# Stores of the result begun by SP, behind the restack of the same slot, instead of by ScalarE

## The reference

```python
x = x + _L0_conv_ref(_gn(x), weight_int8, scale_weight, bias)       # quantized 3x3 convolution
x = x + _L1_conv_ref(_gn(x), w_real, w_imag, b_real, b_imag)        # in _L1: X = rfftn(x), 3x3 complex
                                                                    # convolution of X, bias, irfftn
```

## Time and profile before

| | |
|---|---|
| runs | 3467.41, 3472.81, 3480.56 us, median 3472.81 |
| profiled execution | 3469.19 us, of which 3467.5 us from the first to the last instruction |
| PE busy | 3194.4 us (92%) |
| DVE busy | 2965.4 us (86%) |
| ACT busy | 1908.3 us (55%), without the time its sequencer spends on DMAs |
| POOL busy | 2004.5 us (58%) |
| granted TensorE clock, mean | 0.962 of 2.4 GHz |

### The profile page before, as it was taken

One profiled execution on the slowest core, in us unless ns is written; L12 is line 12 of the kernel. 1 busy time (PEld: TensorE's weight loads), 2 busy tenths in 40 slices (PEclk: granted clock), 3 DMA queues, 4 the chain that ended last, 5 costly groups with the idle time before them and its releaser, 6 DMA issues.

```text
span 3467.5 us, 125723 instructions
## 1 busy us (share of the span) xinstructions
PE 3194.4 (92%) x45156; PEld 2630.8 (76%) x45156; DVE 2965.4 (86%) x5369; ACT 1908.3 (55%) x2831; POOL 2004.5 (58%) x2961
## 2 busy tenths in 40 slices
PE   6988884799999999999999999999999999999998
PEld 3544442488888888888888888888888888888888
DVE  7999998688888888888888888888888888888886
ACT  7999996344444444444444444444444444444443
POOL 3777400256666666666666666666666666666654
PEclk8999997799999999999999999999999999999999
DMA  8777763267777777777767777777777777777765
GB/s 309 245 244 243 240 240 99 67 208 213 211 212 211 217 213 221 215 214 218 217 210 217 216 216 211 219 213 213 220 214 212 212 219 215 212 210 216 218 192 179
DMA packets 545362, 735.72 MB, mean 212 GB/s; under 512 B 80272, under 2 KB 485872, under 8 KB 529296
## 3 DMA queue, kind: packets, MB, share of 16 engines
q1 hardware_dynamic: 351248, 467.90, 40.9%
q0 software_dynamic: 46080, 125.89, 13.8%
q10 hardware_dynamic: 147456, 134.28, 13.6%
HBM read 266.07 MB, written 135.79 MB: 116 GB/s over the span
## 4 chain that ended last, share of the span: by engine, by line
PE 52%; DVE 16%; DMA 6%; issue 5%; SPq 3%; POOL 1%; ACT 0%; DVEq 0%; ACTq 0%; POOLq 0%
PE y_ps L1084 15%; PE x_ps L1071 8%; PE conv_ps L1116 7%; PE fin_ps L1103 6%; DMA stack<-xn 6%; PE t_ps L1062 4%; DVE img L916 4%; SPq L513 3%; PE conv_ps L1118 3%; PE fin_ps L1098 2%; DVE y_lo L909 2%; PE mean_b L1127 2%; DVE img L926 2%; DVE xn L903 1%; DVE bn L918 1%
## 5 line engine op out<-in xcount | busy, mean ns | idle before, releaser
L601 ACT ACTIVATE xt<-t_ps 128x512 f32<-128x512 f32 x512 | 305.7, 597 | 999.4 <-PE t_ps L1062 910.2
L1084 PE MATMUL y_ps<-mix_w,stack 128*128 128x64 f16 x24576 | 811.7, 194 | 18.8 <-DMA stack<-xn 18.1
L1084 PEld LDWEIGHTS y_ps<-mix_w,stack 128*128 128x128 f16 x24576 | 792.7, 99 | 36.0 <-DMA stack<-xn 26.6
L794 POOL DMA_DIRECT2D img<-in_x x960 | 530.3, 553 | 462.0 <-DMA out<-img 404.8
L804 POOL TENSOR_SCALAR eo<-img,norm 128x256 f32<-128x256 f32 x512 | 477.9, 933 | 368.2 <-PE t_ps L1062 200.5
L916 DVE SCALAR_TENSOR_TENSOR img<-conv_ps,cst,img 128x512 f32<-128x512 f32 x512 | 383.2, 748 | 221.6 <-PE conv_ps L1118 216.4
L1071 PE MATMUL x_ps<-dft,xt 128*128 128x128 f32 x4096 | 562.1, 282 | 0.0
L1071 PEld LDWEIGHTS x_ps<-dft,xt 128*128 128x128 f32 x4096 | 518.5, 199 | 0.0
L594 ACT ACTIVATE scaled<-img,b,a 128x512 int16<-128x512 f32 x512 | 412.3, 805 | 96.7 <-DMA img<-in_x 40.8
L1103 PE MATMUL fin_ps<-inv,y_hi 128*128 128x128 f16 x4096 | 461.2, 222 | 0.0
L1116 PE MATMUL conv_ps<-quant,conv_w 128*128 128x512 f16 x1536 | 422.1, 384 | 34.8 <-DVE quant L897 25.7
(11 more groups left out here) (146 smaller groups left out, 5187.6 us busy)
## 6 DMA issues: line engine op xcount, KB each, us to landing
stack<-xn SPq DMA_DIRECT2D x2048, 132.0 KB, 3.3
out<-img ACTq DMA_DIRECT2D x1024, 128.0 KB, 3.4
img<-in_x SPq DMA_DIRECT2D x120, 1024.0 KB, 4.9
img<-in_x POOLq DMA_DIRECT2D x960, 128.0 KB, 3.4
halo<-quant SPq DMA_DIRECT2D x192, 193.3 KB, 4.2
halo<-quant SPq DMA_DIRECT2D x64, 169.1 KB, 3.9
img<-in_x SPq DMA_DIRECT2D x64, 128.0 KB, 2.7
kept<-rmx SPq DMA_DIRECT2D x32, 48.0 KB, 4.5
```

Of the source, the lines that this page charges most:

```text
L794: pool.dma_start(img[u][:, hb, :], src[:, :, hb, :]).then_inc(pair_s[u][j], 16)
L1084: last = nc.tensor.matmul(y_ps[t % 2][:, g, b, :], stack[:, t % 2, g, first:first + F], mix_w[:, 2 * at + b, g, f, part, :], start=i == 0, ...
```

## The change

The procedure `store` moves from ACT's program to SP's, unchanged but for the engine. In a slot it stands last, after that slot's restack; in the next slot halo rows, where there are any, come after it and before the next restack. Waits, destinations, sizes and semaphores are the same.

```diff
@@ SP
+            def store(s, u, t):
+
+                sp.wait_ge(done_s, done(s, t))
+                sp.sem_inc(tick_s, 1)
+                dst = out[s].rearrange("c (h r) w -> c r h w", r=R)
+                for hb in (2 * t, 2 * t + 1):
+                    sp.dma_start(dst[:, :, hb, :], img[u][:, hb, :]).then_inc(store_s[t % STORES], 16)
...
                     if runs(mix, conv, t + 3):
                         restack(s, t + 3)
+                    if mix and t >= 1:
+                        store(s, u, t - 1)
+                    if later(s, mix) and t == 0:
+                        store(s - 1, 1 - u, PAIRS - 1)
...
             periods(sp, period)
+            store(samples - 1, 1, PAIRS - 1)
@@ ACT
-            def store(s, u, t):
-
-                act.wait_ge(done_s, done(s, t))
-                act.sem_inc(tick_s, 1)
-                dst = out[s].rearrange("c (h r) w -> c r h w", r=R)
-                for hb in (2 * t, 2 * t + 1):
-                    act.dma_start(dst[:, :, hb, :], img[u][:, hb, :]).then_inc(store_s[t % STORES], 16)
...
-                    if mix and t >= 1:
-                        store(s, u, t - 1)
-                    if later(s, mix) and t == 0:
-                        store(s - 1, 1 - u, PAIRS - 1)
...
             periods(act, period)
-            store(samples - 1, 1, PAIRS - 1)
```

## The result

The changed kernel takes 3641.44 us (median of 3 runs, 3633.74 to 3642.38) against 3472.81: ratio 1.0477, 95% interval [1.0438, 1.0515]. It is slower by 168.6 us, where 4 were forecast and the range ended at 3512.

A forecast was written before the change was run, and what follows sets the result against it. PE was taken as the bound (92% busy), with little waiting within reach. Terms -4 + 9 - 5 + 4 = +4 us on the profiled 3469.2 gave 3473; runs' median stands 3.6 higher, so 3477 us, range 3450 to 3512.

The forecast's parts named there:

- SP becomes the bound in the halo slots: Rival, chance 0.33: restacks of slots 4 and 8 land 1.2 us late and SP carries the rest along; +35 us, 3508.
- In a quiet slot ... 4.4, against 4.71: it fits: SP's slots without halo rows: restack plus two store issues need 3.9 to 4.4 us, within PE's 4.71 us slot.
- The halo slots: SP's slots with halo rows: next restack starts 1.2 us later, landing put at 0.3 us later, giving +9 us.
- 31 waits: PE's waits for restacks, taken to show about half of such places, 62 over 31 samples, have no slack.
- In such slots the gain is nothing: ACT's sequencer, freed of 1.27 us a slot: PE's wait covers it; gain only once a sample, -4 us.
- +9 us and -5 us, the transfers: Restacks on SP's queue: +9 us from later landings behind halo rows, -5 us where they lose the store as rival.
- +4 us, bounds 0 and +25, for later loads: Stores landing 2.2 to 3 us later delay POOL's loads and ACT's scaled; +4 us was to reach PE.
- ACT's own idle time covers that: ACT's 1.82 us idle a slot was to absorb scaled's waits for late loads of some tenths to 1 us.
- The signs given: Profile signs: PE's stack wait 15 to 30 us if right, over 40 in many slots if wrong on the slow side.
- B: Theory tested in the follow-ups, not forecast: the stores' data stand in SP's queue ahead of the restacks.
- A: Theory tested in the follow-ups: SP's issue time is used up, so restacks and halo rows start late.
- C: Theory tested in the follow-ups: later stores make loads late, and so ACT's scaled and DVE's quant.

The follow-up runs named there:

- one-DMA store: Changed kernel with each store on SP as one DMA of 256 packets, result rows permuted: 3533.7 us; 3474.4 when loads also wait for no store.
- a dose of 270 us of waits: Kernel before, with POOL's loads also waiting for ACT's x_high of pair t+2: 3578.2 us, ratio 1.0294.
- four small DMAs: Kernel before, with four extra DMAs of 16 x 1 KB on SP behind each restack, stores still on ACT: 3889.3 us, ratio 1.1194.
- late loads: Kernel before, with POOL's load also waiting for the mixing of its slot: 3738.0 us, ratio 1.0769.
- three and four small DMAs: Kernel before, with three or four extra DMAs of 16 x 1 KB on SP behind each restack: 3685.95 us with three, 3889.3 with four.
- free loads: Stores read a constant and POOL waits for done_s, so no load waits for a store: 3452.5 us with stores on ACT, 3592.2 on SP.
- the faster version: Kernel before, with ACT's store called one place earlier, ahead of y_high: 3449.9 us, ratio 0.9924.

## Why the prediction was wrong

The direction was that of the rival *SP becomes the bound in the halo slots*, whose 3508 us was too small as well. Its mechanism, late halo slots carried along by SP, was in the main the right one, though it too left out the wait for halo rows; its size was not. Point by point:

- **"In a quiet slot ... 4.4, against 4.71: it fits"** is the step that failed. The sum left out most of SP's own steps. In the rows above the restack is followed by 0.34 us (0.26 in the median), not 0.05, a figure for which no row stands, and a further 0.25 us pass before the next restack: 2.77 + 0.34 + 1.39 + 0.25 = 4.75 us. The pair of stores took 1.38 us in the median, not 1.27. Over the loop a slot in which SP had no pause lasts 4.82 us, not 4.4. These steps are not busy time and stand in no row of an engine, but the earlier trace rows had one: 1756.89 - 1756.70 = 0.19 us between restack and halo rows. The one-DMA store (0.77 us less: 1.39 of the rows above against 0.62) brings that slot to 4.27 us and 139.7 us of loss to 21.9; that is the evidence. A resource needed for 4.82 of 4.71 us carries each delay on, instead of absorbing it in the next slot. (That the wait for `done_s` is free held: 97% of the pauses between restack and store stayed under 0.5 us.)
- **The halo slots** were costed for the restack only (1.2 us later). For one halo slot that was about right: 5.93 us between the restacks, 1.2 over PE's slot. With the lateness carried into it, the restack stood 2.1 us later behind its mixing than before in slot 4 (2.68 against 0.54) and 2.6 in slot 8 (3.38 against 0.77). Nor do the "31 waits" say that half of these places have no slack: of the 31 only 11, with 5.3 of the 18.1 us, are for restacks of slots 4 and 8. And the halo rows also start behind the store, and the convolution of the next slot waits for them: 54.7 us in the change, 82.5 where no load was late. The prediction has them end at 1759.4, later than before, and puts no price on it. I had asked what is queued behind the new wait and stopped at the next restack, though the queue's order has the halo rows first.
- **"In such slots the gain is nothing", -4 us for ACT** was about right as far as it was tested: 0.6 of ACT's 1.27 us less in each slot was worth 0 (ratio 0.9997).
- **+9 us and -5 us, the transfers.** Restacks did land sooner after their issue (median over the span 2.6 us against 3.3, stores 3.0 against 3.4), as forecast for a queue with no rival beside it. It did not matter: they were issued later by more. The other half of that step, shorter issues once ACT's are gone, did not come in the halo slots for which it was counted: the four issues of slot 4's restack take 3.11 us before and 3.10 after (medians). Over all slots they take 2.78 and 2.55. The restack issues of the changed kernel, beside the earlier trace rows:

```profile
L521 SPq DMA_DIRECT2D stack<-xn x2048: 529/600/2303, 669.1 to 3618.1; - x187
```

  600 ns against 606 in the median, 2303 against 2297 at most. What makes the issues of slot 4 long was not found; it is not ACT's stores. The lock on the descriptor generator, which the prediction had cited from the Trainium skill (Perfetto Trace Analysis, "DMA Instruction — HWDGE (DVE, Sync)"), can at most explain the 0.23 us between those two medians of all slots.
- **+4 us, bounds 0 and +25, for later loads** was mis-sized. The mechanism was right, ACT's wait went from 40.8 to 149.5 us. Inside the change it cost 28.9 us (give or take 18), and 39 (give or take 13) where SP was hardly in its way; a dose of 270 us of waits cost +103. "ACT's own idle time covers that" held for ACT, not for DVE, whose wait for `scaled` rose by 89 us.
- **The signs given** were met on the slow side: a `stack` wait over 40 us (79.3), the halo restack late, by 2.1 us instead of 1.2, loads and stores waited for more, the statistics' wait unchanged at 65.3 us.
- **Why the parts don't add.** PE's 4.71 us slot, SP's 4.82 and DVE's (2104 of 2465 us busy) lie close together. When SP makes PE late by a microsecond, a load gets that microsecond too; this is my reading. That both costs hide each other partly is measured: +415 us with four small DMAs, +264 with late loads, +463 with both.

What stays open: 41.4 us of the loss are PE's busy time, which did not rise at all with free loads (3201.8 and 3202.2 us). Late loads are not needed for such a rise: with three and four small DMAs, where the loads were not late, PE was busy for 3247.2 and 3303.4 us, 52.8 and 109 more than before. The mean granted clock was 0.954 in the change, 0.952 and 0.943 in those two, 0.962 before, and 0.959 and 0.963 with free loads. A clock of 0.954 in place of 0.962 would make 27 us of the 41.4, if all of PE's busy time went with it (an estimate, 3194.4 x 0.962 / 0.954 - 3194.4). What lowered it was not isolated, nor is it sure that the 28.9 us of the late loads hold none of it. Nor was B alone measured; after A and C there is little left for it, as the one-DMA store with free loads is within 22 us of its base with all the data in SP's queue. The Trainium skill (DMA: Bandwidth & Descriptors, "Issuing engines are not separate DMA queues") says that starting DMAs on several engines saves only sequencer time, which is usually small beside the DMA. These runs agree with the first half. The second is not so here: the 1.39 us of issuing two stores stand beside 3.0 us until one has landed, and on SP they were worth 139.7 us.

## What to carry to other kernels

Before you move a DMA, write the receiving sequencer's whole slot: from the start of one group of DMAs to the start of the next, gaps and waits included, and set it against the slot of the busiest engine. Here 4.82 us against 4.71 cost 139.7 us, and 4.27 still cost some 22; nothing between was measured. Where it comes near the other slot, count it as full, and count every delay in the longer slots as carried on until the next slot with room. Then list everything that is queued behind the moved DMA, with the first reader of each, not only the one that is waited for today. And a buffer's store, its reload and the reload's first use are one chain: moving the store's start by some microseconds is felt where the reload is used, so look for the earliest place where the store can be issued (here ahead of `y_high`, worth 0.8%).

## What the runs showed of the hardware

- A DMA's price on SP hardly went by its packets: medians of 616 ns for 256 rows of 1 KB, 597 for 128, and 371 or 340 (three or four a slot) for 16. Merging two DMAs of 128 rows took SP's time for a store from 1.38 to 0.62 us.
- In the loop of the changed kernel SP let at least 0.25 us pass between a restack and a store, in either order, and at least 0.19 between halo rows and a restack, also in slots where the mixing that it waits for had ended 2 us before. How much of this is the wait's own cost no run here separates.
- 128 writes of 4 bytes in a DMA, two DMAs a slot, made the load packets of another queue hold the DMA engines 2.6 times as long (1247 against 478 us), and the store packets of a third 1.35 times (639 against 472).
- DVE's `quant`, one instruction of fixed size, took 278 ns at least and on average 473 before, 562 in the change and 361 in the faster version:

```profile
L897 DVE TENSOR_SCALAR quant<-scaled 128x512 f16<-128x512 int16 x512 | 242.0, 473 | 52.0 <-ACT scaled L594 50.5 <-issue 0.3
```

```profile
L897 DVE TENSOR_SCALAR quant<-scaled 128x512 f16<-128x512 int16 x512 | 184.7, 361 | 56.3 <-ACT scaled L594 55.2 <-issue 0.3
```

  The first is the kernel before, the second the faster version. With free loads it is 341 and 345 ns, whichever engine stores. In 860 to 3325 us of the changed kernel 105 of 423 executions took over 700 ns, all of them at least partly beside a two-operand fold of POOL, and of the 318 shorter ones 82; before it was 87 of 448, in the faster version 32 of 451. A likely reading is that the folds fall elsewhere in the slot when the loads don't hold POOL back; it was not tested. The Trainium skill (GPSIMD Engine Reference, "Specifications") says that GpSimd shares its SBUF interfaces with VectorE, with contention for VectorE's instructions that are in a two-port mode or have two SBUF inputs. The overlap agrees with that, if `quant` is in such a mode, which no run here shows; that this is the cause was not tested apart. If it is, it is a cost of a late store that reaches DVE by no wait at all.
